# An attention kernel on one core: the Gram products of a head moved ahead of the score products in each slot of TensorE

## The reference

```python
q, k_t, v_t = heads(x @ W_q), heads(text @ W_k), heads(text @ W_v)       # text: the first 252 rows of the context
probs_t = softmax(q @ k_t.T * scale)                                     # per head, 256 x 252
text_out = probs_t @ v_t
qsem = l2norm(probs_t @ text)                                            # per head, 256 x 512
sem = qsem @ l2norm(ip).T                                                # ip: the last 4 rows of the context
probs_ip = softmax(q @ k_ip.T * scale + 0.5 * sem) * spatial_mask
out = (text_out + probs_ip @ v_ip) @ W_out + b_out + x
```

## Time and profile before

| | us |
|---|---|
| median of 3 runs | 1654.78 (1651.68 to 1661.64) |
| the profiled execution | 1654.13 |
| its span, first to last instruction | 1652.3 |
| PE busy in the span | 1585.6 (96%) |
| DVE busy | 1376.9 (83%) |
| ACT busy | 990.9 (60%) |
| POOL busy | 841.0 (51%) |

### The profile page before, as it was taken

How to read it: one execution, slowest core, us unless ns; L and a number is a source line. 1 busy time by engine, 2 the same in 40 slices (tenths; PEclk the granted TensorE clock), 3 DMA queues, 4 the chain that set the end, 5 groups by cost and what they waited for, 6 DMA issues and landing times.

```text
span 1652.3 us, 42210 instructions
## 1 busy us (share of the span) xinstructions
PE 1585.6 (96%) x14152; PEld 1409.6 (85%) x14152; DVE 1376.9 (83%) x3937; ACT 990.9 (60%) x2044; POOL 841.0 (51%) x789
## 2 busy tenths in 40 slices
PE   6999999999999999998999999999999999999986
PEld 5888888888888888778888989998899989888965
DVE  4687788888888888876879998999999999999985
ACT  3465555656655565654656666666666666666652
POOL 3234432222233222434767776767776777777663
PEclk9999999999999999998999999999999999999998
DMA  8334444444444444543333323332333323332211
GB/s 225 98 106 122 120 124 127 130 121 124 124 128 122 125 128 124 149 120 88 89 102 94 99 69 102 102 104 78 98 95 102 97 78 103 109 96 67 81 30 43
DMA packets 204224, 175.29 MB, mean 106 GB/s; under 512 B 45441, under 2 KB 203531, under 8 KB 204011
## 3 DMA queue, kind: packets, MB, share of 16 engines
q1 hardware_dynamic: 204010, 172.60, 36.5%
HBM read 112.13 MB, written 60.38 MB: 104 GB/s over the span
## 4 chain that ended last, share of the span: by engine, by line
PE 87%; DVE 6%; issue 3%; ACT 1%; DMA 1%; SPq 1%; POOL 1%; DVEq 0%; POOLq 0%; ACTq 0%
PE MISC L103 26%; PE GP L103 20%; PE NAT L265 10%; PE TR L278 8%; PE PV L324 5%; PE PV L309 4%; PE PV L306 3%; PE PV L327 2%; PE MISC L227 2%; DVE ZP L895 1%; PE MISC L368 1%; PE MISC L466 1%; DVE TMP L779 1%; PE MISC L367 1%; PE MISC L388 1%
## 5 line engine op out<-in xcount | busy, mean ns | idle before, releaser
L540 ACT ACTIVATE P<-TA 128x512 f32<-128x512 f32 x320 | 202.3, 632 | 279.0 <-DVE TA L888 277.6
L984 POOL TENSOR_TENSOR ZS<-ZP 128x256 f32<-128x256 f32 x267 | 253.5, 949 | 205.1 <-DVE ZP L895 204.1
L265 PE MATMUL NAT<-KS,QS 65*128 65x256 f32 x1280 | 300.2, 317 | 3.9 <-DMA KS<-qk_parts 2.5
L103 PE MATMUL GP<-PH,GH 128*128 128x256 f32 (+1 forms) x960 | 248.3, 288 | 21.1 <-DVE ZP L895 20.1
L278 PE MATMUL TR<-QS,KS 69*128 69x256 f32 (+1 forms) x1280 | 260.4, 285 | 4.8 <-DVE TA L888 2.7
L783 DVE TENSOR_REDUCE MX<-NAT 128x2 f32<-128x504 f32 x320 | 216.4, 676 | 53.3 <-PE NAT L265 48.9
L901 DVE SCALAR_TENSOR_TENSOR PM<-P,PH 128x512 f32<-128x512 f32 x320 | 254.8, 796 | 0.0
L215 POOL TENSOR_TENSOR PARTS<-QKF,PARTS 112x508 fp32r<-112x508 f32 (+3 forms) x93 | 119.1, 1280 | 265.0 <-ACT PARTS L568 263.1
L265 PEld LDWEIGHTS NAT<-KS,QS 65*128 65x128 f32 x1280 | 201.2, 192 | 57.1 <-issue 42.6
L103 PE MATMUL GP<-PH,GL 128*128 128x256 f32 (+1 forms) x960 | 242.5, 281 | 0.0
L543 ACT ACTIVATE P<-TR 128x512 f32<-128x512 f32 x320 | 192.4, 601 | 72.3 <-PE TR L278 69.2
(11 more groups left out here) (253 smaller groups left out, 3846.4 us busy)
## 6 DMA issues: line engine op xcount, KB each, us to landing
QS<-qk_parts SPq DMA_DIRECT2D x480, 64.0 KB
KS<-qk_parts SPq DMA_DIRECT2D x480, 64.0 KB
qk_parts<-PARTS SPq DMA_DIRECT2D x128, 224.0 KB, 2.8
CT<-in_ctx_t SPq DMA_DIRECT2D x32, 512.0 KB, 3.9
qk_parts<-PARTS SPq DMA_DIRECT2D x64, 192.0 KB, 2.4
XT<-in_x_t SPq DMA_DIRECT2D x48, 112.0 KB, 2.6
XT<-x_t SPq DMA_DIRECT2D x48, 112.0 KB, 2.4
XB<-in_x SPq DMA_DIRECT2D x16, 320.0 KB, 4.1
```

What stands on the lines that cost most here:

```text
L103: ins = e.matmul(out, lhs, rhs, start=(n == 0), stop=(n == len(pairs) - 1))
L265: ins = e.matmul(NAT[s % 2][:, i * T:(i + 1) * T], QS[0:KQ, h, i * 128:(i + 1) * 128], KS[0:KQ, h, :], start=True, stop=True)
L540: e.activation(P[:, s % NP, :], TA[:, s % 2, :], ACT.Exp, scale=SCALE).then_inc(q["exp"], 1)
L984: e.tensor_tensor(ZS[s % NZ][:, :], ZP[:, s % 2, 0:S], ZP[:, s % 2, S:2 * S], ALU.add).then_inc(q["zs"], 1)
```

## The change

In TensorE's loop the block of the Gram products (head t - 2) moves from behind the two score products to in front of them. A slot's order becomes GP (head t - 2), NAT (head t + 11), TR (head t), PV if due, MISC. No instruction, wait, buffer or DMA is added or taken away, and the other four programs stay as they are.

```diff
                 ins.then_inc(q["stm"], 1)
-            s = t + LEAD
-            if 0 <= s < 2 * S1:
...
-                for i in range(2):
-                    ins = e.matmul(NAT[s % 2][:, i * T:(i + 1) * T], QS[0:KQ, h, i * 128:(i + 1) * 128],
-                                   KS[0:KQ, h, :], start=True, stop=True)
-                ins.then_inc(q["nat"], 1)
-            s = t
-            if 0 <= s < 2 * S1:
...
-                ins.then_inc(q["tr"], 1)
             s = t - 2 - S1
             if 0 <= s < S1:
                 b, h = divmod(s, H)
...
                 e.wait_ge(q["ph"], s + 1)
                 if s:
                     e.wait_ge(q["zp"], s)
                 p0, p1 = PH[:, k, 0:S], PH[0:N2, k, S:2 * S]
                 product(e, GP[:, 0:S], [(GH[:, p, 0, :], p0), (GL[:, p, 0, :], p0)])
                 product(e, GP[:, S:2 * S], [(GH[:, p, 1, :], p0), (GL[:, p, 1, :], p0), (GH[0:N2, p, 2, :], p1),
                                             (GL[0:N2, p, 2, :], p1)]).then_inc(q["gp"], 1)
+            s = t + LEAD
+            if 0 <= s < 2 * S1:
...
+                ins.then_inc(q["nat"], 1)
+            s = t
+            if 0 <= s < 2 * S1:
...
+                ins.then_inc(q["tr"], 1)
             g = due_group(t, HG + 1, 0, G1)
```

More of the change, by code:

```diff
@@ L252, in _ @@
                 ins.then_inc(q["stm"], 1)
+            s = t - 2 - S1
+            if 0 <= s < S1:
+                b, h = divmod(s, H)
+                p, k = b % 2, s % NS
+                if s == 0 and ring.freed[2]:
+                    e.wait_ge(*ring.freed[2])
+                if h == 0:
+                    e.wait_ge(q["gl"], 3 * (b + 1))
+                e.wait_ge(q["ph"], s + 1)
+                if s:
+                    e.wait_ge(q["zp"], s)
+                p0, p1 = PH[:, k, 0:S], PH[0:N2, k, S:2 * S]
+                product(e, GP[:, 0:S], [(GH[:, p, 0, :], p0), (GL[:, p, 0, :], p0)])
+                product(e, GP[:, S:2 * S], [(GH[:, p, 1, :], p0), (GL[:, p, 1, :], p0), (GH[0:N2, p, 2, :], p1),
+                                            (GL[0:N2, p, 2, :], p1)]).then_inc(q["gp"], 1)
             s = t + LEAD
@@ L280, in _ @@
                 ins.then_inc(q["tr"], 1)
[L281 to L295, removed]
             g = due_group(t, HG + 1, 0, G1)
```

## The result

The changed kernel takes 1798.19 us (median; 1790.81 to 1800.71) against 1655.57 us before: ratio 1.085, 95% interval 1.082 to 1.089. The forecast was 1789 us, the range 1740 to 1838. The profiled execution took 1800.59 us, so 146.5 us more than the profiled one of before are to be found.

The account below looks back on a forecast made before the run. TensorE was taken to bound the kernel; a new loop with VectorE would add 123 us in 273 regular slots and 11 us in the first 36, 134 us in all, giving 1789 us, range 1740 to 1838.

Parts of the forecast that it names:

- The bound before: Whole kernel before the change: TensorE bounds it, busy 96% of the span, with 87% of the chain on it.
- The loop: Layer two, between TensorE and VectorE: ZP, GP, NAT, MX, ZP takes 3.10 us per slot, against 2.70 today.
- ZP to GP: In each layer-two slot, from ZP's start on VectorE to GP's start on TensorE: 0.82 us.
- GP to NAT: On TensorE in each layer-two slot, from GP's start to NAT's start: 0.75 us, bounds 0.71 and 0.79.
- NAT to MX: In each layer-two slot, from NAT's start on TensorE to MX's start on VectorE: 0.51 us.
- MX to ZP: On VectorE in each layer-two slot, MX's start to ZP's start, small pieces between: 1.02 us on average.
- late PMs: On VectorE between ZP and the next MX: two long PMs in 20 slots, up to 0.4 us each, 0.04 a slot.
- the last step: MX start to ZP start on VectorE: POOL's stretching of L826 and L853 stays; otherwise 1759 us or 1822 us.
- The regular slots: Layer two, 273 slots after the first 36: 3.15 us each instead of 2.70, 123 us in all.
- The first 36 slots: Start of layer two: 0.3 us more each, between 0.1 and 0.45, 11 us; their own stalls hide part of the loop.
- Rival 2: Regular part of layer two: TensorE's clock halves for two slots in twenty, some 35 us more, 1824 us; chance 0.10.
- What would show it: Signs in the profile after: 17 ZPs in 54 us, clock 1.00, GP and MX waiting in nearly every slot.

Follow-up runs that it names:

- e2: TensorE's slot order set to TR, GP, NAT instead of the changed kernel's GP, NAT, TR; 1794.89 us, ratio 1.084 to the kernel before.

## Why the prediction was right, step by step

- **The bound before** (TensorE, by the chain) held: 77 us of added TensorE work cost 51 us there and 21 in the changed kernel.
- **The loop** ZP, GP, NAT, MX, ZP is shown by its two exits: NAT in front of GP (1670 us) or ZP in front of MX (1665 us) opens it, and with TR in front of GP it stays closed (1795 us). That TR costs some 14 us of its own behind GP was not foreseen; the prediction had it hidden, since PH is wanted only two slots on.
- **Its steps.** ZP to GP: 0.82 forecast, 0.86 measured. GP to NAT: 0.75, 0.80; the upper bound of 0.79 was the right one, since GP waits in nearly every slot and the slow second matmul comes each time. NAT to MX: 0.51, 0.53. MX to ZP: 1.02, 0.94. The sum 3.10 became 3.12: three steps were forecast a little short and the last too long, and they cancelled. That is luck in part. The measured steps hold besides what the forecast put on top of the loop: TensorE's longer slots (8 of 128, the ones above) and late PMs.
- **A slip in the last step.** The 20 distances from MX to ZP that the prediction adds up, from 1216.1 us on, come to 21.0 us and not 20.4, so this step was 1.05 and not 1.02 in the kernel before. With it the same working gives some 9 us more, 1798 us. The step then fell by 0.11 us, and the slip covered part of that.
- **The last step** was the one whose price was said to hang on POOL, and the prediction kept the stretches whole. The stretched L826 went from a median of 1448 ns to 977 ns, and the longest L853 from 1360 to 646 ns. The operations of L826 in the changed kernel (ns min/median/max), then one of them with the POOL operation beside it, and then the one of the kernel before beside the CTSL of the earlier trace rows:

```profile
L826 DVE TENSOR_TENSOR FU<-ON,NRM x16: 311/977/998, 897.1 to 1784.1; 128x160 f32<-128x160 f32 x16
...
1207.80 2.55 POOL L1027 TENSOR_TENSOR CTSL<-CT,CTSH 128x1024 fp32r<-128x1024 f32 x1
1209.55 0.98 DVE L826 TENSOR_TENSOR FU<-ON,NRM 128x160 f32<-128x160 f32 x1
...
1248.94 1.46 DVE L826 TENSOR_TENSOR FU<-ON,NRM 128x160 f32<-128x160 f32 x1
```

So what the stretch adds to the shortest L826 fell by about two fifths (1.13 to 0.66 us); it neither stayed nor went. The rows show what sets it. CTSL ended at 1210.35 and L826 at 1210.53 in the changed kernel, 1250.22 and 1250.40 in the kernel before. In all 13 cases before and all 10 after in which L826 starts beside a CTSL, it ends 0.18 or 0.19 us behind it; in the others it takes 0.31 to 0.33 us. Its length is thus what is left of CTSL when it starts, and the change let it start later in CTSL. The forecast tied it to POOL's queue and not to this overlap.
- **The late PMs** (0.04 us a slot) were priced as staying, and nearly all went: 34 of 320 PMs took over 1 us in the kernel before, 6 in the changed one.
- **The regular slots**: 273 x 0.45 = 123 us forecast; 272 slots grew by 123.0 us. That the two agree to the microsecond is chance, as the slip, the shorter stretches, the missing late PMs and TR's 14 us show.
- **The first 36 slots** are where most is missing. The profiled execution came out 12.6 us above the 1788 forecast for it, and 9.5 of these are here: 11 us forecast, 20.5 measured, 0.57 a slot where I had bounded it at 0.45. The reason given (stalls of their own under which the loop disappears) had the wrong sign for the clock. The granted clock in these two stretches went from 0.97 and 0.94 to 0.87 and 0.87. TensorE was busy 95.4 us of these 108 instead of 98.1, and it ran more of the start at 1.2 GHz, where NAT and GP in the loop take twice as long. Over the 36 slots the mean granted clock was 0.95 before and 0.86 after, that is some 10 us at 1.2 GHz before and 38 after; with 0.95 us more for each slot of about 4.1 us the added 28 us are an estimate of 6 us, more than the excess over the bound (4.3 us). e2, which has the same loop, points the same way: clock 0.91 over its first 36 slots, and 125.2 us. But TR stands elsewhere there, so it is no clean test of the clock, and none was made.
- **Rival 2** (the clock falls in the regular part) held in a small way: 0.99 from 900 to 1500 us and 0.98 over the 272 regular slots, less than half of two slots in twenty. It fell more at the start, as said above. The Trainium skill, TensorE: Matmul & The Clock Gate, "What's actually happening", says that the gate is set by how busy the engine has been recently; the traces agree as far as the changed kernel and the one before go (0.99 with 542.5 us of busy PE in 600, 1.00 with 596.8 us in the kernel before). They do not when the run with all pieces behind ZP is taken in (0.98 with 583.4 us).
- **What would show it**: 17 ZPs in 54 us was met, MX waiting for NAT was met (over 100 us forecast from 900 to 1500 us; 141.6 us), PE was busy 90% instead of near 85%, and DVE 75% instead of near 80%, since its stretched pieces got shorter. GP's waiting in nearly every slot was met by its hand-over from ZP (120 slots of 128), and not by the table's label (79 entries for ZP, 48.2 us); PE's idle time, 57 us in 600, is within the 50 to 90 us forecast. The clock was to be 1.00 and was 0.99. The share of DVE in the chain came to 13% and not 30%: the page's share is over the whole span, of which layer one is nearly half, and in layer two the chain goes to ScalarE in some slots by the name shown above.

## What to carry to other kernels

When two engines hand work to each other through one buffer, write down the loop, that is, the list of what stands between one use of the buffer and the next on both engines, in the order of their queues; a block that moves ahead of another on one engine can put a third piece of work into that loop without any new wait in the code. Change the order on both sides together: the same TensorE order cost 8.5% with VectorE's old order and 0.6% with the matching one. In a loop that binds, a piece costs most of its length (17 us came back for two pieces of some 1.5 us in 20 slots). Further on in the same queue it is free as long as the engine would wait there; with all pieces moved there VectorE came late, and a quarter to two fifths of the gain expected did not come.

## What the runs showed that was not expected

- The table of waits can name the wrong releaser in a steady pattern: 172 entries named PH, and a kernel with PH delayed by a whole copy had GP start in the middle of a copy in 43 slots of 125. Compare the release with the usual hand-over (here 0.14 to 0.15 us from the end of ZP to GP) before believing a name.
- The granted clock from 900 to 1500 us was 0.99 in the changed kernel and 0.98 in the one with all pieces behind ZP, although TensorE was busy 542.5 us in the first and 583.4 us in the second. No run separates why.
- A DVE instruction beside a POOL instruction was stretched by what was left of the latter: L826, with some 0.32 us alone, took 0.98 or 1.45 us by when it started beside CTSL, and ended 0.18 or 0.19 us behind CTSL in all 23 cases of the two kernels. Such a stretch moves with the timing alone, so it is to be priced as a range.
- A run's total can hide two effects of opposite sign: e2 stood 3 us under the changed kernel, 10 us longer in layer one and 14 us shorter behind it. Compare by stretch before saying that a block's place does not matter.
